# Attention over a paged cache: four page buffers in place of three, fewer heads of Wo ahead of time, and the weights scaled on GpSimd

## What is computed

```python
q = rope(rmsnorm(x @ Wq.T))                  # 32 heads of 128
k = rope(rmsnorm(x @ Wk.T)); v = x @ Wv.T    # 8 heads of 128
kc = k_cache[block_table]; vc = v_cache[block_table]   # 16 pages of 32 keys per sequence
k_all = concat(kc, k); v_all = concat(vc, v)           # 512 + 32 keys
scores = q @ k_all.T * SCALE; scores = where(valid, scores, -1e30)
x = x + (softmax(scores) @ v_all).reshape(64, 32, 4096) @ Wo.T
```

## Time and profile before

| what | value |
|---|---|
| runs | 2223.37, 2230.19 and 2231.25 us, median 2230.19 |
| the profiled execution | 2221.79 us, its span 2220.0 us |
| TensorE busy | 2152.6 us (97%) |
| VectorE busy | 1462.8 us (66%) |
| ScalarE busy | 1392.3 us (63%) |
| GpSimd busy | 220.3 us (10%) |
| attention | about 541 to 1660 us of the span |

### The profile page before, as it was taken

How to read it: one execution, slowest core, us unless ns; L and a number is a source line. 1 busy time by engine, 2 the same in 40 slices (tenths; PEclk the granted TensorE clock), 3 DMA queues, 4 the chain that set the end, 5 groups by cost and what they waited for, 6 DMA issues and landing times.

```text
span 2220.0 us, 77529 instructions
## 1 busy us (share of the span) xinstructions
PE 2152.6 (97%) x30576; PEld 1647.3 (74%) x30576; DVE 1462.8 (66%) x3642; ACT 1392.3 (63%) x4174; POOL 220.3 (10%) x208
## 2 busy tenths in 40 slices
PE   8999999999999999999999999999999999999998
PEld 6888888887666766667676676676777888888886
DVE  5799999994566766667676666666764433433433
ACT  4888888884677777777777777777773222222221
POOL 5211111110000111100000000000003101101101
PEclk9999999999999999999999999999999999999999
DMA  5455545548999999999999999999984333333331
GB/s 193 104 131 113 115 110 117 132 97 272 359 338 319 324 330 317 312 321 329 334 323 319 323 309 328 314 316 308 335 295 145 107 90 101 107 95 101 98 101 50
DMA packets 355010, 490.22 MB, mean 221 GB/s; under 512 B 58994, under 2 KB 191346, under 8 KB 351987
## 3 DMA queue, kind: packets, MB, share of 16 engines
q1 hardware_dynamic: 354674, 485.62, 68.3%
HBM read 397.37 MB, written 88.08 MB: 219 GB/s over the span
## 4 chain that ended last, share of the span: by engine, by line
PE 94%; issue 2%; SPq 2%; DMA 1%; DVE 1%; ACT 1%; ACTq 0%; DVEq 0%
PE o_bank L971 25%; PE s_bank L951 23%; PE acc L730 8%; PE acc L731 8%; PE acc L732 8%; PE proj L1408 5%; PE proj L1410 5%; PE proj L1409 5%; PE wide L1455 1%; PE wide L1450 1%; PE slim L1439 1%; PE wide L1451 1%; PE turn L1429 1%; PE slim L1437 1%; DMA kv<-k_spill 0%
## 5 line engine op out<-in xcount | busy, mean ns | idle before, releaser
L971 PEld LDWEIGHTS o_bank<-p_t,kv 32*128 32x128 f32 x17408 | 519.5, 187 | 134.0 <-issue 132.8
L898 DVE CUSTOM_DVE_ANT_0 probs<-s_bank,mask 128x544 f32<-128x544 f32 x512 | 370.7, 725 | 356.3 <-PE s_bank L951 356.3
L971 PE MATMUL o_bank<-p_t,kv 32*128 32x128 f32 x17408 | 574.8, 277 | 23.5 <-issue 22.7
L951 PE MATMUL s_bank<-kv,q_t 128*32 128x288 f32 (+1 forms) x8192 | 531.3, 397 | 22.7 <-issue 20.6
L856 ACT ACTIVATE probs<-probs,neg_max 128x544 f32<-128x544 f32 x512 | 383.4, 752 | 258.5 <-DVE neg_max L898 246.7
L951 PEld LDWEIGHTS s_bank<-kv,q_t 128*32 128x32 f32 x8192 | 247.7, 110 | 217.1 <-issue 32.4
L912 DVE STREAM_TRANSPOSE p_t<-probs 128x544 f32<-128x544 f32 x512 | 365.3, 731 | 0.4 <-ACT probs L862 0.4
L862 ACT ACTIVATE probs<-probs,inv_sum 128x544 f32<-128x544 f32 x512 | 356.8, 751 | 0.0
L730 PE MATMUL acc<-w_hi,x_hi 128*128 128x512 f32 x764 | 300.5, 393 | 0.0
L731 PE MATMUL acc<-w_lo,x_hi 128*128 128x512 f32 x764 | 300.1, 393 | 0.0
L732 PE MATMUL acc<-w_hi,x_lo 128*128 128x512 f32 x764 | 298.1, 390 | 0.0
(11 more groups left out here) (137 smaller groups left out, 2466.7 us busy)
## 6 DMA issues: line engine op xcount, KB each, us to landing
kv<-in_kv_pages SPq DMA_DIRECT2D x1024, 256.0 KB, 4.6
q_spill<-stage SPq DMA_DIRECT2D x512, 64.0 KB, 1.8
q_t<-q_spill SPq DMA_DIRECT2D x64, 512.0 KB, 5.8
o_spill<-o_t SPq DMA_DIRECT2D x64, 512.0 KB, 6.6
raw<-o_spill SPq DMA_DIRECT2D x64, 512.0 KB, 3.5
kv<-in_w_qkv SPq DMA_DIRECT2D x11, 1024.0 KB, 5.8
v_spill<-stage SPq DMA_DIRECT2D x8, 1024.0 KB, 7.1
k_spill<-stage SPq DMA_DIRECT2D x128, 64.0 KB, 1.8
```

Source lines behind the costliest of these rows:

```text
L898: nc.vector.tensor_tensor_reduce(out=probs[:, i], in0=s_run(n), in1=mask[:, b % 2], scale=-SCALE, scalar=3.0e38, op0=ALU.add, op1=ALU.min, ...
L951: last = pe.matmul(s_banks[n % 2][rows, columns].rearrange("p (s t) -> p s t", t=PSIZE), q_t[:, b % 2, g, r * S:(r + 1) * S], kv[:, buf, s ...
L971: last = pe.matmul(o_banks[a][:, hh * ROWS:(hh + 1) * ROWS], kv[rows, buf, c, VALUES + hh * HD:VALUES + (hh + 1) * HD], p_t[rows, m % 2, c ...
```

## The change

- `BUFS` is 4 and the buffer of batch b is b % 4. The memory for the fourth comes from Wo: `WO_EARLY` is 8, `HI_EARLY` is 6, and `stage` of the projection lies where `wo_early` does. What lay after the first buffer in `finish` is laid out anew.
- SP's loop in `attend`: iteration b waits for the sums of batch b-4, issues pages, own keys and own values of batch b, then the queries of batch b-1, four heads of Wo (b is 4 or 5), and the store of batch b-4. The queries of the last batch follow the loop.
- GpSimd multiplies the weights by the inverted sums, and no longer ScalarE. It splits the six early heads in between, in batches 9 to 14.
- `finish` splits 13 pieces in place of 8, and the chunks of the output stand after the fifth and the ninth.

```diff
-BUFS = 3
+BUFS = 4
-WO_EARLY = 16
-HI_EARLY = 16
+WO_EARLY = 8
+HI_EARLY = 6
 def buf_of(b):
-    return (b + BUFS - 1) % BUFS
+    return b % BUFS
...
-        x_lo = nc.alloc_sbuf_tensor_at("x_lo", [P, DC, TOK], F32R, offset=wo_start)
+        x_lo = nc.alloc_sbuf_tensor_at("x_lo", [P, DC, TOK], F32R, offset=kv_start + buf_of(3) * SLOTS * PAGE * 4)
+        stage = wo_early[:, :, :].rearrange("p h n -> p (h n)").rearrange("p (i n) -> p i n", i=2)
...
-        WO_WITH = {b: HS * (b - 2) for b in range(2, 2 + WO_EARLY // HS)}
+        WO_WITH = {b: HS * (b - BUFS) for b in range(BUFS, BUFS + WO_EARLY // HS)}
...
-            load_pages(sp, 2)
             for b in range(2, B):
                 if b == BUFS:
                     for i in range(2):
                         sp.wait_ge(stored[i], 16 * (NV + (NQ + NK) * NT) * (NT // QUARTER) // 2)
                 if b >= BUFS:
                     sp.wait_ge(summed, 4 * (b - BUFS + 1))
-                if b > 2:
-                    load_pages(sp, b)
+                load_pages(sp, b)
                 load_own_keys(sp, b)
                 load_own_values(sp, b)
-                sp.wait_ge(scored, (b - 1) * HK)
-                load_queries(sp, b)
+                if b > 2:
+                    sp.wait_ge(scored, (b - 2) * HK)
+                    load_queries(sp, b - 1)
...
                 if b >= BUFS:
                     store(b - BUFS)
+            sp.wait_ge(scored, (B - 2) * HK)
+            load_queries(sp, B - 1)
+            store(B - 4)
             sp.wait_ge(summed, 4 * (B - 2))
             load_late(sp)
...
         def _(pool):
+            def normalise(n):
+                i = n % SLOTS_P
+                pool.wait_ge(inverted, n + 1)
+                nc.gpsimd.tensor_scalar(probs[:, i], probs[:, i], inv_sum[:, i:i + 1], None, ALU.mult).then_inc(normed, 1)
...
-            for h in range(HI_EARLY):
-                pool.wait_ge(normed, (SPLIT_FROM + h) * HK + 2)
-                upper_weights(h)
-                pool.wait_ge(normed, (SPLIT_FROM + h) * HK + 6)
-                lower_weights(h)
+            for n in range(UNITS):
+                normalise(n)
+                h, step = n // HK - SPLIT_FROM, n % HK
+                if 0 <= h < HI_EARLY:
+                    if step == 1:
+                        upper_weights(h)
+                    if step == 5:
+                        lower_weights(h)
...
         def _(act):
-                if t > 0:
-                    normalise(2 * t - 2)
-                    normalise(2 * t - 1)
                 weigh(2 * t)
                 weigh(2 * t + 1)
-            normalise(UNITS - 2)
-            normalise(UNITS - 1)
...
-        CHUNK_AFTER = {FIRST_PIECE + 3: 2, FIRST_PIECE + 5: 3}
+        CHUNK_AFTER = {FIRST_PIECE + 4: 2, FIRST_PIECE + 8: 3}
```

More of the change, by code:

```diff
@@ L154, in decoder @@
             x1 = after("x1", [P, D])
-            assert place[0] <= kv_start + BUF_BYTES
             o_hi_done, o_split = sem("o_hi_done"), sem("o_split")
-            place = [kv_start + BUF_BYTES]
-            o_hi = nc.alloc_sbuf_tensor_at("o_hi", [P, 2, CH, P], F32R, offset=place[0])
-            place[0] += 2 * CH * P * 4
             wr_a = after("wr_a", [P, DC, E + ER])
@@ L164, in decoder @@
             w1, w1_lo = after("w1", [P, DC, D], "w1_lo")
+            up2, up2_lo = after("up2", [2 * LOWS, D], "up2_lo")
+            assert place[0] <= kv_start + 2 * BUF_BYTES
+            place = [kv_start + 2 * BUF_BYTES]
+            o_hi = nc.alloc_sbuf_tensor_at("o_hi", [P, 2, CH, P], F32R, offset=place[0])
+            place[0] += 2 * CH * P * 4
             o_lo = nc.alloc_sbuf_tensor_at("o_lo", [P, 2, CH, P], F32R, offset=place[0])
             place[0] += 2 * CH * P * 4
-            up2, up2_lo = after("up2", [2 * LOWS, D], "up2_lo")
-            assert place[0] <= kv_start + 2 * BUF_BYTES
             early_bytes = place[0] - q_start
@@ L281, in project @@
         part_s = sb("part_s", [P, 2, HS, HD])
-        stage = sb("stage", [P, 2, QUARTER * SLICE])
         angle, turns = (buf[:, :, :, :].rearrange("p i h d -> p (i h d)").rearrange("p (t n) -> p t n", n=HALF)
@@ L857, in weigh @@
                                      accum_out=row_sum[:, i:i + 1]).then_inc(weighed, 1)
[L859 to L862, removed]
             def evacuate(b):
```

## The result

The changed kernel takes 2231.99 us (median of 20 runs) against 2221.5 us for the kernel before (20 runs): 1.0044 times as long, 95% interval 1.0028 to 1.0059, or +9.8 us. I had said +6.5 us and "within 0.5%". The execution profiled has a span of 2232.7 us, 12.7 more than the one before. The 9.8 us of the medians are what is to be explained; the trace shows where its own 12.7 lie.

What follows compares the result with a forecast made beforehand. The prediction took TensorE to be the limit, its attention idle time coming from late queries and, by inference, late instruction blocks. Terms 6.0 + 0 + 0 + 0.5 = +6.5 on a 2230.2 us median gave 2236 us, range 2219 to 2248.

Steps and rivals of the forecast that it cites:

- The steady state of the four buffers: Attention's later batches: queries keep their release and distance, so the fourth buffer changes the time by 0.
- sum for the lateness: Batch starts: pages to queries 13.7, table load 1.8, landing 5.8, together 21.3 us against 20.4 available, so queries sometimes late.
- The start: First batches of attention: queries of batch 2 go out behind batch 3's pages; +6.0 us, bounds 3.5 and 10.0.
- GpSimd: cost: Scaling weights in attention: 0.75 us per multiplication, at most 1.37, fits the period; cost 0, drain -0.2 to +1.3.
- Wo: Projection after attention: larger late load just under cover, thirteen pieces split in place of eight; +0.5 us, bounds 0 and 3.
- The sum: Whole kernel: the terms add up to +6.5 us.
- The ten stalls go: Rival, batch starts in attention: pages come last and now have slack; -12.7 + 6.5 gives 2224 us; chance 0.12.
- all idle time goes: Rival, attention: all TensorE idle time goes and the start costs nothing; -38.3 gives 2192 us; chance 0.07.
- the 38.3 us: TensorE's idle time in the attention window: 12.7 at ten batch starts, 25.6 mostly inside runs of equal matmuls.
- GpSimd becomes the bound: Rival, attention: two multiplications per period decide from 2.1 us each; at 2.3 each +59, 2296 us; chance 0.07.
- The start is not made up for: Rival: the start's 10 us stay, late load, pieces and mask builds add; +12 to +18, 2242 to 2248 us; chance 0.18.

Runs made afterwards that it cites:

- e2: The changed kernel with the queries of batch b-1 issued ahead of the pages of batch b in every iteration: 0.9946 of the kernel before.
- e6: The kernel before, three buffers, with the queries issued ahead of the pages from batch 3 on: 0.9913 of the kernel before.
- e12: The changed kernel with SP's loop put back to three batches ahead, queries of batch b behind its pages: 1.0011 of the kernel before, 2223.2 us.
- e5: The changed kernel loading only a quarter of each page's columns from batch 4 on: 0.9943 of the kernel before, 2211.3 us.
- e1: The changed kernel with only the queries of batch 2 issued ahead of the pages of batch 3: 1.0047 of the kernel before.
- e3: The changed kernel with the weights scaled by ScalarE again: 1.0062 of the kernel before.
- e4: The kernel before with only the scaling of the weights moved to GpSimd: 1.0019 of the kernel before.
- e7: The changed kernel with an unread 128x512 copy on GpSimd ahead of each multiplication: 1.0164 of the kernel before, 2258.3 us from two runs.
- e8: The kernel of e2 with the weights scaled by ScalarE: 0.9940 of the kernel before.

## Why the prediction was right

**The steady state of the four buffers: right.** SP's loop is the old one with later pages in it. Nine batch starts after batch 6 stall behind queries issued 4.5 to 6.5 us before, 9.3 us together (forecast: 10 to 16, of the same kind), against ten and 12.7 before. A tenth stall, 1.9 us before batch 62, is of another kind: its queries had landed 3.1 us earlier, and what it waits for isn't shown. e2 and e6 show that it is the order that matters: put ahead of the pages, the queries no longer stall anyone, with four buffers or with three. The fourth buffer buys nothing that a time here shows; in the traces it saves at most e6's three waits for own keys, 2.2 us, which e2 doesn't have. The prediction's sum for the lateness (21.3 us against 20.4) took 13.7 us from an early iteration; with the median of 12.65 it is 20.2, and so the queries are late only at times.

**The start: right in place and size, with one reason too many.** Forecast +6.0 (3.5 to 10.0), batch 2 at 586; measured +6.6 at batch 6, batch 2 at 585.14. Taking the run-ahead back (e12) brings batch 6 back to 647.1 and lowers the ratio by 0.0033, some 7 us. Two misses offset each other in the 586: SP issued the queries 2.8 us earlier than I had added up (577.62, not 580.4), and they took 7.4 us to land, not 5.8. What I had left open was what the lost time consists of: I named both SP's 16.4 us per iteration and the full DMA engines. e5 speaks for SP: a quarter of the bytes from batch 4 on shortens neither SP's way to the queries nor the lateness of batch 6. e1 shows that moving one transfer forward doesn't help as long as one more iteration of SP stands ahead of what is due. That the time isn't regained later fits the steady loop, in which the same queue is only just in time; no run tests this by itself.

**GpSimd: cost right at 0 in the stage, its price wrong.** I took 0.75 us and bounded it by 0.65 and 1.37; it is 1.64. The row of a cast did not stand for a multiplication, and the row of a two-input subtraction was no upper bound. The step held because the slack (3.3 us for one, 4.0 for two) had room for 3.3; the margin was 0.7 us, not the 2.5 that I thought. At the drain it costs 0.4 us in this pair of traces and 0 to 0.7 over all kernels, within my bounds of -0.2 and +1.3; in the times e3 and e4 can't tell it from 0. VectorE is not disturbed: the transposes have a median of 0.739 us, before 0.732. Nor is the one instruction that could use both ports, the mask build, held up. The timeline of one period:

```profile
1006.34 1.64 POOL L840 TENSOR_SCALAR probs<-probs,inv_sum 128x544 f32<-128x544 f32 x1 [2.17 <-DVE inv_sum L904]
1006.85 0.48 DVE L888 TENSOR_SCALAR mask<-key_index,seq_f 128x512 f32<-128x512 f32 x1
```

It starts while GpSimd is at work, runs beside it, and takes 0.48 us, 12 ns more than before. Of the 64 mask builds 63 lie wholly inside one of GpSimd's multiplications, and none takes over 0.489 us. The exclusion that the Trainium skill ("SBUF — State Buffer", Who interferes with whom) gives for a two-port instruction does not show for this pair: the mask build's time, below one cycle per column at that engine's 0.96 GHz by "VectorE: DVE Perf Modes" (Specifications), suggests that mode, but it neither waited nor was stretched. The figures of the Trainium skill ("GPSIMD Engine Reference", Elementwise — side-by-side cycle accounting) for one-input and two-input work, from which I had an estimate of 0.47 or 1.18 us of loop, come near the product of two tensors (1.12 us) and not near TENSOR_SCALAR (1.57 to 1.66), which has one tensor input.

**Wo: within its bounds.** The first result of the stage behind stands 40.5 us after its first matmul, against 40.3 before; but against the kernels with sixteen split heads whose attention was otherwise altered (38.1 in e4, 38.6 in e6) it is 2 us more. Forecast +0.5, bounds 0 and 3. The larger late load stayed under cover: it landed at 1658.1, 19.9 us after its issue (forecast 23.1), and the first projection matmul begins at 1668.8.

**The sum.** 6.5 forecast, 9.8 measured (6.2 to 13.1 by the interval). Where the other 3 us come from isn't shown. What e12 leaves of the loss, 1.0011, is the drain, Wo and all else together, and its interval holds 1. The forecast time of 2236 us came closer to the measured 2232 than the terms deserve: it stood on a median of 2230.2 for the kernel before, from three runs, which is 2221.5 over twenty, so a base 8.7 us too high hid a change that I had put 3.3 us too low.

**The rivals.** "The ten stalls go" and "all idle time goes" are out for this change, though e2 shows that the first was there to be had by another edit. Of the 38.3 us, the part in the middle of runs needs less DMA traffic (e5), not deeper buffers. "GpSimd becomes the bound" happens at 2.29 us per unit (e7) and not at 1.64. "The start is not made up for" (+12 to +18) is out as it stood: of the 9.0 us at batch 2 6.6 were left at batch 6, and neither the late load nor the mask builds show a cost.

What stays open: why e2, e6 and e8 gain 18 to 20 us between batches 6 and 62 where the stalls they remove sum to 9 to 13; six traces of kernels with the old order differ by up to 19 us there (955 to 975), so one trace does not settle it. Nor was it shown directly that the late arrivals in mid-run are instruction blocks; e5 shows only that they go with the DMA load.

## What to carry to other kernels

Write down for each transfer how long before its use it is issued and what stands ahead of it on its queue: one more buffer helps only the transfer that comes last, and here the pages got a batch of slack while the queries, issued behind them, got none. The remedy was to issue first what is due first, with the buffers as they were (0.9913). The issuing engine's time per transfer is a budget of its own: pages, own keys and own values, 21 transfers, took 13.2 us (median) with pages of 64 KB and 12.6 with pages of 256. Running one batch further ahead puts one such iteration ahead of the first queries that are due, which cost 9.0 us at batch 2 and 6.6 at batch 6.

## What the runs showed of the hardware

On GpSimd a TENSOR_SCALAR over 128x544 float32 takes 1.64 us, with a constant 1.57, where a TENSOR_TENSOR with a broadcast operand takes 1.12 and a copy of 128x512 takes 0.63. A VectorE TENSOR_SCALAR of 128x512 took 0.48 us inside GpSimd's TENSOR_SCALAR 63 times, and 0.47 without one. SP's issue of sixteen 64 KB transfers took 10.0 us (median, 8.7 to 11.7), as long as that of sixteen 256 KB ones (9.7, 8.7 to 11.7), with the DMA engines at half their load. After TensorE had stood still for 9.8 us its granted clock was 0.50 until 589.6, and 32 score matmuls took 3.85 us in place of 2.04.
